# Decoder block on one core: v's copy and normalise on ScalarE, v's bias behind attention, one split on GpSimd, a new order

## What is computed

```python
def _layernorm(x, axis=-1, eps=1e-05):
    ...
    return (x - m) / jnp.sqrt(v + eps)
...
x = _layernorm(x + attn(x, W_qkv, b_qkv, W_proj, b_proj))       # causal self attention
x = _layernorm(x + xattn(x, ctx, ctx, mask, wq, bq, wk, bk, wv, bv, wo, bo))
x = _layernorm(x + ffn(x, ...))
...
attn = jax.nn.softmax(attn, axis=-1)
z = jnp.einsum('bhqk,bhkd->bhqd', attn, v)                      # v = x @ W + b_v
return z @ W_proj + b_proj
...
# ffn: attention without an output projection, plus 8 experts, the top two of a gate
expert_out = jnp.einsum('bsd,edf->bsef', x, W_experts) + b_experts
moe_out = jnp.einsum('bsef,bse->bsf', expert_out, combine)
return attn_out + moe_out
```

## Time and profile before

| what | value |
|---|---|
| median of 3 runs | 971.46 us (968.36 to 973.17) |
| the profiled execution | 970.37 us, span 968.7 us |
| mean granted PE clock | 0.985 of full speed |
| instructions | 28521 |

### The profile page before, as it was taken

How to read it: one execution, slowest core, us unless ns; L and a number is a source line. 1 busy time by engine, 2 the same in 40 slices (tenths; PEclk the granted TensorE clock), 3 DMA queues, 4 the chain that set the end, 5 groups by cost and what they waited for, 6 DMA issues and landing times.

```text
span 968.7 us, 28521 instructions
## 1 busy us (share of the span) xinstructions
PE 885.6 (91%) x9964; PEld 743.2 (77%) x9964; DVE 862.8 (89%) x3931; ACT 530.4 (55%) x1083; POOL 409.7 (42%) x490
## 2 busy tenths in 40 slices
PE   5798999998889999999999999999999999999986
PEld 3787888787878888888887777777778777777774
DVE  4799999999889999989898789998888888888985
ACT  4576767666657676767676444444344434444422
POOL 5678878786664444444444222211222122212200
PEclk8999999999999999999999999999999999999999
DMA  5565555554434534343433222222222222222210
GB/s 176 159 176 165 139 157 155 163 163 131 130 83 129 148 105 129 106 128 106 128 96 106 68 67 77 63 69 71 78 73 62 66 67 79 78 78 78 61 29 23
DMA packets 98161, 100.87 MB, mean 104 GB/s; under 512 B 10700, under 2 KB 90596, under 8 KB 98020
## 3 DMA queue, kind: packets, MB, share of 16 engines
q1 hardware_dynamic: 98020, 99.05, 36.8%
HBM read 18.53 MB, written 4.19 MB: 23 GB/s over the span
## 4 chain that ended last, share of the span: by engine, by line
DVE 43%; PE 35%; issue 9%; ACT 5%; DMA 4%; POOL 2%; SPq 1%; DVEq 0%; POOLq 0%; ACTq 0%
PE work L477 15%; DVE x_all L999 7%; DVE max_scores L918 6%; PE work L607 6%; DVE neg_max L921 6%; PE max_scores L562 4%; PE scores L586 4%; PE work L616 3%; DVE neg_max L918 2%; DVE combine_first L901 2%; ACT attn L767 2%; DVE z L942 2%; DVE x_all L973 2%; DVE bn_stats L955 2%; DVE x_all L1011 1%
## 5 line engine op out<-in xcount | busy, mean ns | idle before, releaser
L918 DVE CUSTOM_DVE_ANT_0 max_scores<-max_scores,mask_qk 128x128 f32<-128x128 f32 x1024 | 260.6, 324 | 16.9 <-PE max_scores L562 16.1
L767 ACT ACTIVATE attn<-scores 128x512 f32<-128x512 f32 x384 | 215.2, 597 | 105.8 <-PE scores L586 101.0
L562 PE MATMUL max_scores<-k_stack,q_stack 126*128 126x128 bf16 x1536 | 148.7, 222 | 12.2 <-DVE neg_max L918 8.7
L586 PE MATMUL scores<-q_stack,k_stack 128*128 128x128 bf16 x1536 | 142.3, 222 | 9.4 <-DMA q_stack<-neg_max_t 4.9
L918 DVE DVE_READ_ACCUMULATOR2_ANT neg_max<- 128x1 f32 x1024 | 142.7, 139 | 0.0
L1038 POOL TENSOR_TENSOR q_full<-q_full,q_parts 128x512 f32<-128x512 f32 x48 | 56.9, 1184 | 183.9 <-ACT q_parts L725 183.9
L562 PEld LDWEIGHTS max_scores<-k_stack,q_stack 126*128 126x128 bf16 x1536 | 99.9, 98 | 45.2 <-issue 18.4
L999 DVE SCALAR_TENSOR_TENSOR x_all<-work,combine,x_all 128x256 f32<-128x256 f32 x256 | 122.6, 479 | 6.9 <-PE work L477 1.6
L477 PE MATMUL work<-split_hi,w_hi 128*128 128x256 f32 x384 | 118.6, 309 | 8.2 <-DVE split_lo L820 8.2
L586 PEld LDWEIGHTS scores<-q_stack,k_stack 128*128 128x128 bf16 x1536 | 97.9, 98 | 33.8 <-ACT attn L767 12.3
L607 PE MATMUL work<-attn,v_ones 128*32 128x128 f32 x3072 | 103.8, 275 | 19.5 <-DVE x_all L999 17.1
(11 more groups left out here) (115 smaller groups left out, 2013.2 us busy)
## 6 DMA issues: line engine op xcount, KB each, us to landing
k_stack<-k_parts SPq DMA_DIRECT2D x288, 128.0 KB, 2.4
q_stack<-q_parts SPq DMA_DIRECT2D x288, 128.0 KB, 2.4
in_t<-in_xt SPq DMA_DIRECT2D x16, 256.0 KB, 3.0
x_all<-in_x SPq DMA_DIRECT2D x16, 256.0 KB, 3.0
in_t<-in_ct SPq DMA_DIRECT2D x16, 256.0 KB, 3.5
...
```

Source lines behind the costliest of these rows:

```text
L562: mm = pe.matmul(dst[:, b, h2, :], head(QS, n, 2 * p + h2, b, ROWS), head(KS, n, 2 * p + h2, b, ROWS), start=(b + h2 == 0), stop=(b + h2 = ...
L586: mm = pe.matmul(dst[:, b, h2, :], head(KS, n, 2 * p + h2, b, rows), head(QS, n, 2 * p + h2, b, rows), start=(b + h2 == 0), stop=(b + h2 = ...
L767: act.activation(attn("exp", n, p)[:, :, :], SS[g % 2][:, :, :, :].rearrange("k b h q -> k (b h) q"), ACT.Exp).then_inc(probs_done, 1)
L918: ins = dve.tensor_tensor_reduce(scores, scores, MQ[l][:, :], -1.0, HUGE, ALU.add, ALU.min, NM[n % 2][:, b, h:h + 1])
```

## The change

**Normalise on ACT.** `normalise` leaves DVE's list and enters ACT's: Identity with scale = rstd and bias = -mean x rstd, a pointer each. POOL makes the bias: two operations on 2 columns per pair more (`neg_mean`, `neg_mean_rstd`), and one wait more in the chain of the power.

**v's copy.** In layers 0 and 1 ACT copies v of both sequences in one instruction (`v_copy`, kind "va"), without a bias. In layer 2 DVE still copies it, now without the bias row, and still adds the gate's bias row to the logits.

**v's bias behind attention.** In layers 0 and 1 PE multiplies the bias of v by the output weights once per layer (`output_bias`, kind "bo": four fp32 matmuls), and DVE adds that to the output's bias row (`bias_sum`, "bor"). In layer 2 it becomes two more rows of the experts' biases, 26 rows for 24, with weight 1. The bias rows shrink from 1288 to 520 columns; DVE's setup gets three more small memsets and two more waits.

**The context's low part.** `c_low` leaves DVE's list and enters POOL's.

**The table.** All times are new; the periods are 16.5, 18.14 and 25.14 (16.5, 18.13, 24.96 before).

```diff
-PERIOD = [16.5, 18.13, 24.96]
+RB_O = [0, D]
+RB_GATE = 2 * D
+RB_COLS = 2 * D + E
+PERIOD = [16.5, 18.14, 25.14]
 TIMES = [
...
-     "sum": [22.73], "rs": [23.43], "norm": [25.72]},
+     "sum": [22.71], "rs": [22.58], "norm": [25.25], "va": [-19.61]},
...
+BIAS_TIMES = [(-14.0, -12.5), (130.0, 132.0)]
...
+            def output_bias(l, part):
...
+                for c in range(C):
+                    for k, w in enumerate((WH[l], WL[l])):
+                        mm = pe.matmul(dst[:, 0:D], COLB[:, l, 2, c:c + 1].to_broadcast([P, P]),
+                                       w[:, c, 3 * D:4 * D].bitcast(F32), start=(c + k == 0), stop=(c + k == C))
...
+            def v_copy(n, part):
+                act.wait_ge(v_psum[0], n + 1)
...
+                if n >= VALUES:
+                    act.wait_ge(pv_psum, PV_TURN[(n - VALUES, 1)] + 1)
+                act.activation(VA[n % VALUES][:, :, 0:H * VH].rearrange("p b (h d) -> p b h d", h=H)[:, :, :, 0:DH],
+                               bank("v", n)[:, :].rearrange("p (b h d) -> p b h d", b=PB, h=H), ACT.Copy).then_inc(va_done, 1)
+
+            def normalise(n, part):
+                l, x = layer(n), pair(n)
+                act.wait_ge(rs_done, n + 1)
+                for b in range(PB):
+                    ins = act.activation(x[:, b, :], x[:, b, :], ACT.Identity, bias=SHIFT[:, l, b:b + 1], scale=RS[:, l, b:b + 1])
+                ins.then_inc(norm_done, 1)
...
-            def c_low(n, part):
-                split_free(dve, "c", n)
...
             def v(n, b):
...
-                    dve.tensor_tensor(GL[:, b, :], src[:, D:VG], RB[:, RB_V[2] + D:RB_V[2] + VG], ALU.add)
...
+                dve.tensor_tensor(GL[:, b, :], src[:, D:VG], RB[:, RB_GATE:RB_GATE + E], ALU.add)
+                dve.tensor_copy(VA[n % VALUES][:, b, 0:H * VH].rearrange("p (h d) -> p h d", h=H)[:, :, 0:DH],
+                                src[:, 0:D].rearrange("p (h d) -> p h d", h=H)).then_inc(v_done[b], 1)
...
+            def bias_sum(l, part):
+                bias = RB[:, RB_O[l]:RB_O[l] + D]
+                dve.wait_ge(bo_psum, l + 1)
+                dve.tensor_tensor(bias, bank("bo", l)[:, 0:D], bias, ALU.add).then_inc(bo_done, 1)
...
-            def normalise(n, part):
-                l, x = layer(n), pair(n)
-                dve.wait_ge(rs_done, n + 1)
...
+            def c_low(n, part):
+                split_free(pool, "c", n)
+                pool.wait_ge(ch_done, turn(n))
...
             def rstd(n, part):
                 l = layer(n)
                 pool.wait_ge(mv_done, n + 1)
-                pool.tensor_tensor(VE[:, l, :], MV[:, l, :, 1], EPSC[:, :], ALU.add).then_inc(ve_done, 1)
+                pool.tensor_tensor(VE[:, l, :], MV[:, l, :, 1], EPSC[:, :], ALU.add)
+                pool.tensor_tensor(NEG[:, l, :], ZERO[:, :], MV[:, l, :, 0], ALU.subtract).then_inc(ve_done, 1)
                 pool.wait_ge(ve_done, n + 1)
-                pool.tensor_tensor(RS[:, l, :], VE[:, l, :], NHALF[:, :], ALU.pow).then_inc(rs_done, 1)
+                pool.tensor_tensor(RS[:, l, :], VE[:, l, :], NHALF[:, :], ALU.pow).then_inc(power_done, 1)
+                pool.wait_ge(power_done, n + 1)
+                pool.tensor_tensor(SHIFT[:, l, :], NEG[:, l, :], RS[:, l, :], ALU.mult).then_inc(rs_done, 1)
```

122 lines of the change are left out of this document (64 added, 58 removed), and 46 rows, old and new, of the table TIMES.

## The result

The changed kernel takes **940.65 us** (median of 4 runs, 939.32 to 941.35) against 971.73 for the kernel before on the same chip (968.36 to 973.17): a ratio of 0.9683, 95% interval 0.9656 to 0.9711. The forecast was 941. The total agrees and its parts do not: layer 2 gave almost everything, and layers 0 and 1 together gave next to nothing.

The account below looks back on a forecast made before the run. Layer 0 was held bound by DVE, layer 1 by PE, layer 2 by both waiting on each other; -14.1 - 4.8 - 11.2 - 0.7 = -30.8 us from 971.5 gave 941 us, range 926 to 960.

Parts of the forecast that it names:

- the mis-sized term: Layer 2: 0.65 us for normalise plus 0.9 for the collision minus 0.7 idle, taken as 0.8 x 14 pairs = 11.2 us.
- I take half, 0.9 us: Layer 2: half the time per pair lost where POOL's work on q meets L901 and L907 would return, 0.9 us.
- So I charge 0.7 us of new idle time: Layer 2: z of the first half, now ahead of the expert bias, makes DVE wait 0.7 us more per pair.
- My upper end: Layer 2: the most gained if PE never waits, 1.9 us per pair x 14 = 26.6 us.
- I take 14.0, near PE's row: Layer 0: new period 14.0 us, 0.88 us less per pair, 14.1 us over 16 pairs.
- what a lighter DVE can return is the 0.32 us that are idle: Layer 1: only PE's idle 0.32 us per pair can come back, taken as 0.3 x 16 = 4.8 us.
- the rival on a blocked ACT: Layers 0 and 1: normalise in ACT's queue waits for late POOL operations and delays what follows; 988 us, chance 0.08.
- The activation's price: ACT's normalise in layer 0: two activations at 0.42 us each with overlap, 0.84 us per pair.
- The ends: Kernel's start and tail: 2.0 us back from shorter bias rows, 0.5 lost to new matmuls, 0.8 in the tail; net -0.7.
- POOL or ACT as the bound of layer 0: Rival for layer 0: POOL or ACT limits it, giving only 0.3 us per pair; 950 us, chance 0.12.
- Idle time in layer 2: Rival: collision stays and zT is waited for; layer 2 gives nothing, layer 1 gives 1 us; 956 us, chance 0.12.
- PE's stalls gone: Rival: PE's stalls vanish altogether in layers 1 and 2; 926 us, chance 0.07.

Follow-up runs that it names:

- experiments in 4: Against the changed kernel: ACT's normalise on 2 of 256 columns, 932.78 us; layer 0's normalise back on DVE without POOL's two extra operations, 936.58 us.

## Why the prediction was right in its total and wrong in its parts

**Layer 2, the mis-sized term.** The mechanism was the right one: POOL's work on q over L901 and L907. The step that failed is "I take half, 0.9 us", and the next one, "So I charge 0.7 us of new idle time". The order put POOL's work behind the gate in all twelve steady pairs, and the idle time in front of z's first half cost nothing. Net I took 0.8 us per pair and the mean period fell by 2.41. The kernel before with q later shows that 1.86 of these need no work moved at all, and normalise, which I priced at 0.65, changes nothing when it goes back to DVE in the new order (24.04). My upper end, 26.11 - 24.21 = 1.9, treated PE's busy time before (24.21) as a floor; it held short waits in overlap, and PE gets by with 24.0. It also began from one period, 26.11 us, where the mean of the twelve is 26.42 (the last two take 27.5 and 27.7). The term was -11.2, and between the powers of pairs 31 and 45 (563.65 and 928.15 before, 563.39 and 896.59 after) 31.3 us came.

**Layer 0, the step that failed.** "DVE's period falls from 14.88 to 13.58 us ... I take 14.0, near PE's row, because PE will be next." DVE's busy time did fall to 13.59, and the period stayed at 15.22, with PE at 14.07, ACT at 12.21 and POOL at 12.52. My own condition, over 14.5 us with PE or DVE idle, is met. The sum also began from one period of 14.88 us; the mean of ten is 15.36 (153.63/10), with DVE busy 15.03, so even its start was a short period and not the typical one. No engine's sum fills the new period. ACT's normalise is a part of what does (0.17 us when shortened, 0.25 when it goes back to DVE with POOL's short chain, experiments in 4); that the rest is a round of short waits through the queues is argued and not shown. The old code with the new table, at 14.94, shows that the table helped and the moves took back 0.28. Between the best period of all runs (14.94) and PE's busy time in it (13.79) 1.15 us remain; which queue holds them no run shows, except that in the changed kernel POOL's select doesn't.

**Layer 1, the wrong sign.** "what a lighter DVE can return is the 0.32 us that are idle": the period grew by 0.39 us. The 16.35 us of that row was a longer period than most; the mean of ten was 16.16 already, with 0.21 us of PE idle. Nothing in the text asked what ACT's queue does to PE in this layer, except the rival on a blocked ACT, and this rival asked for the wrong cause, a late POOL. ACT's normalise waits for POOL 7.6 us in all, in 3 waits, at the end of the layers. It is the instruction's own 1.1 us in front of L805 and the next exps that costs, 0.23 to 0.25 of the 0.39 us, and this part vanishes where ACT would idle anyway. The remaining 0.14 us have no cause shown.

**The activation's price.** I took 0.84 us per pair from L717's overlap. The group shows 599 ns for one and 52.4/96 = 0.546 us with overlap, 1.09 per pair. From the figures of the Trainium skill (ScalarE: Activation LUTs, What ACT_TABLE_LOAD costs) the prediction had worked out an estimate of 586 ns for one; the measured 599 are 2% more. The 0.98 us for a pair that I worked out from that page was nearer than my own 0.84, and is what the two take from ACT's queue, from 407.40 to the next start at 408.38 in the timeline above. The sum didn't use this price.

**The ends.** The start was to give 2.0 us and take 0.5 back; the power of pair 1 came 1.2 us earlier (78.29 for 79.46), and DVE's wait for the last constant went from 2.93 to 2.46 us only. The tail's 0.8 us was right: from the last pair's addition on POOL to the end it is 4.35 us before (964.30 to 968.65) and 5.13 now (933.32 to 938.45). The 1.4 us above, behind pair 45, hold the last two pairs too. L917, the copy without a bias row, takes 414 ns, as wide as L879, as I had it.

**The rivals.** POOL or ACT as the bound of layer 0: its gain of 0.3 us a pair was nearer to the measured 0.14 than my 0.88, its cause was not shown: POOL's select holds nothing there, ACT's normalise 0.17 us. Idle time in layer 2: it was there at z's first half, the cost was not. PE's stalls gone: true in layer 2, with a chance of 0.07, and false in layer 1. So 941 came out because an error of 20 us in layer 2 (31.3 for 11.2) was made up by 9 in layer 0 with its border (5.0 for 14.1) and 11 in layer 1 (5.9 us slower for 4.8 faster, by the powers of pairs 15 and 31). That is luck: mistakes that offset each other confirm no step.
